# Joining the moments of two norms on GpSimd, with the square roots, reciprocals and scalings a slot or more later

## The reference

```
x  = x + layernorm(attention(layernorm(x)))        # norms 1 and 2
x  = x + layernorm(spikes(layernorm(x)))           # norms 3 and 4
_layernorm(x) = (x - mean) / sqrt(var + 1e-5)      # over the 256 features
attention: q, k, v = x @ W_qkv.T; k normalised per head (16 values);
           F_t = retention * F_(t-1) + coef * v_t k_t^T;  y_t = (W_LTM + F_t) q_t;  y @ W_o.T
spikes:    y = relu(x @ W_fc.T)^2 @ W_proj.T; five steps of a threshold neuron; spike count / 5
```

## Time and profile before

| | us |
|---|---|
| median of three runs (634.02, 634.74, 641.57) | 634.74 |
| the profiled execution's own time | 633.62 |
| its span, first to last instruction | 631.8 |
| PE busy | 497.6 (79%) |
| DVE busy | 534.2 (85%) |
| ACT busy | 328.7 (52%) |
| POOL busy | 389.0 (62%) |
| mean granted TensorE clock | 0.886 |

### The profile page before, as it was taken

The page is one execution under the profiler, slowest core; times in us unless marked ns, Lnnn a source line. Parts: engine busy times, 40 slices in busy tenths (PEclk is TensorE's granted clock), DMA queues, the critical chain, the costliest instruction groups (busy, mean ns, idle before and its releaser), DMA issues.

```text
span 631.8 us, 7778 instructions
## 1 busy us (share of the span) xinstructions
PE 497.6 (79%) x2264; PEld 325.4 (52%) x2272; DVE 534.2 (85%) x933; ACT 328.7 (52%) x641; POOL 389.0 (62%) x186
## 2 busy tenths in 40 slices
PE   3585548359996999699969997899879996896891
PEld 1341225136673667365736575566646664484670
DVE  4799999997999999999999998999999999712001
ACT  4532113245647754675466636654666455636634
POOL 0048975785567766877687756875787677710201
PEclk9877667659997999899989989799979997978896
DMA  7475566456644774466556653577347844200000
GB/s 238 112 210 144 162 154 186 131 143 160 182 133 116 188 209 137 133 167 200 149 149 152 176 170 107 147 182 206 100 117 202 215 101 133 67 1 0 33 1 33
DMA packets 54730, 87.63 MB, mean 139 GB/s; under 512 B 5409, under 2 KB 19361, under 8 KB 54689
## 3 DMA queue, kind: packets, MB, share of 16 engines
q1 hardware_dynamic: 54112, 87.12, 49.9%
q10 hardware_dynamic: 576, 0.03, 0.1%
HBM read 78.74 MB, written 8.39 MB: 138 GB/s over the span
## 4 chain that ended last, share of the span: by engine, by line
PE 51%; issue 16%; DVE 15%; ACT 10%; POOL 6%; DMA 1%; POOLq 0%; ACTq 0%; DVEq 0%
PE p_c L346 13%; PE p_c L371 12%; DVE state L732 9%; PE p_a L281 6%; PE p_y L324 5%; PE p_c L337 4%; POOL prod L873 3%; ACT sign L547 3%; PE p_c L354 2%; PE p_a L301 2%; POOL x1t L889 2%; DVE p_u L722 2%; PE p_y L319 2%; ACT oo L468 1%; PE p_c L363 1%
## 5 line engine op out<-in xcount | busy, mean ns | idle before, releaser
L873 POOL TENSOR_TENSOR prod<-state,qf 128x1024 f32<-128x1024 f32 x128 | 303.1, 2373 | 140.4 <-DVE state L732 121.9
L732 DVE TENSOR_TENSOR_SCAN state<-ret,p_u 128x512 f32<-128x512 f32 x256 | 309.2, 1209 | 0.0
L722 DVE TENSOR_TENSOR p_u<-vrep,p_k 128x512 f32<-128x512 f32 x256 | 171.5, 676 | 2.5 <-ACT p_k L479 2.5
L346 PE MATMUL p_c<-wproj_sb,ht 128*128 128x256 f32 x512 | 116.1, 382 | 1.3 <-ACT ht L537 1.3
L346 PEld LDWEIGHTS p_c<-wproj_sb,ht 128*128 128x128 f32 x512 | 95.7, 190 | 24.3 <-issue 9.2
L371 PE MATMUL p_c<-x1t,wfc_s 128*128 128x512 f32 x384 | 98.9, 410 | 9.1 <-POOL x1t L889 8.0
L281 PE MATMUL p_a<-xt,wqkv_s 128*128 128x512 f32 x276 | 82.7, 438 | 10.6 <-POOL xt L889 3.0
L371 PEld LDWEIGHTS p_c<-x1t,wfc_s 128*128 128x128 f32 x384 | 73.9, 196 | 31.3 <-POOL x1t L889 12.3
L324 PE MATMUL p_y<-prod,summer 128*32 128x512 f32 x512 | 76.8, 675 | 10.4 <-POOL prod L873 10.4
L281 PEld LDWEIGHTS p_a<-xt,wqkv_s 128*128 128x128 f32 x276 | 53.3, 203 | 45.7 <-issue 16.9
L535 ACT ACTIVATE hr<-p_c 128x512 f32<-128x512 f32 x64 | 38.2, 597 | 34.6 <-PE p_c L371 32.6
(11 more groups left out here) (107 smaller groups left out, 505.2 us busy)
## 6 DMA issues: line engine op xcount, KB each, us to landing
vrep<-v_rows SPq DMA_DIRECT2D x256, 256.0 KB, 3.6
xa<-in_x SPq DMA_DIRECT2D x8, 512.0 KB, 5.3
v_rows<-vf SPq DMA_DIRECT2D x16, 256.0 KB, 2.3
x<-in_x SPq DMA_DIRECT2D x8, 512.0 KB, 4.5
out<-x SPq DMA_DIRECT2D x8, 512.0 KB, 3.3
ht<-in_w_fc SPq DMA_DIRECT2D x1, 1024.0 KB, 7.6
wproj_sb<-in_w_proj SPq DMA_DIRECT2D x1, 1024.0 KB, 10.1
state<-in_w_qkv SPq DMA_DIRECT2D x1, 512.0 KB, 5.8
```

The lines of the kernel that those rows point to most:

```text
L346: last = pe.matmul(p_c[(u + 1) % 2][:, 0:D], ht[:, f, tokens(u)], wproj_sb[:, f, :], start=(f == 0), stop=(f == FT - 1))
L722: v.tensor_tensor(p_u[n % NU][:, :], vrep[:, n % NV, :], p_k[:, :], ALU.mult).then_inc(S["hebb_done"], 1)
L732: v.tensor_tensor_scan(state[:, s % NS, i, :], ret[:, r:r + 1].broadcast_to([P, L]), p_u[n % NU][:, :], 0.0, ALU.mult, ALU.add).then_inc(S ...
L873: p.tensor_tensor(prod[:, s % NZ, :, :], state[:, s % NS, :, :], qf[:, s // HS, :].unsqueeze(1).broadcast_to([P, 2, L]), ALU.mult).then_in ...
```

## The change

For norms 1 and 4 VectorE only takes BN_STATS. GpSimd then joins the halves over all four tiles at once, in new tiles `squares`, `spread` and `twice_mean`: the squares of both halves are added, and 64 times the squared difference of the two means is added to them. This is 256 times the variance, so that ScalarE's square root takes `scale=1/256`. These are five GpSimd instructions of 128x4 values for norm 1 and six for norm 4 (which also keeps the sum of the means); three of them wait for the one before on the semaphore `pool_step`. The spike norm's offsets become two GpSimd instructions, the second of which waits in the same way. Norms 2 and 3 stay as they are.

Moved in the lists, besides:

- GpSimd: `moments_of(1, b)` in slot 1 and `moments_of(4, b2)` in slot 11, ahead of that slot's `read`; `spike_offsets` in slot 13 ahead of the read; `add_feed_forward` from slot 13 to slot 15.
- ScalarE: `deviation(1)` from slot 0 to slot 2, ahead of `copy_y`; `norm1` from 2 to 3; `deviation(4)` from 11 to 12, now behind `hidden(b1, 1)` and `hidden(b1, 2)`; `norm4` from 12 to 14.
- VectorE: `scales(1)` from slot 2 to 3. `scales(4)` stays in slot 12.

```diff
             def deviation(n, b):
                 act.wait_ge(S[f"n{n}_var"], at(b + 1))
-                eps = eps_sb[:, 1:2] if n == 4 else eps_sb[:, 0:1]
-                nc.scalar.activation(dev[n - 1][:, :], moments[n - 1][:, :, 1], ACT.Sqrt, bias=eps).then_inc(S[f"n{n}_dev"], 1)
+                if n in (1, 4):
+                    eps = eps_sb[:, 1:2] if n == 4 else eps_sb[:, 0:1]
+                    nc.scalar.activation(dev[n - 1][:, :], squares[n][:, :], ACT.Sqrt, bias=eps, scale=1.0 / D).then_inc(
+                        S[f"n{n}_dev"], 1)
...
             def norm4(b):
-                act.wait_ge(S["n4_step"], at(2 * (b + 1)))
+                act.wait_ge(S["n4_offset"], at(b + 1))
...
+                        if after: deviation(1, b)
                         if before: copy_y(b1, 1)
                         if now: key_deviation(g, 1)
-                        if after: norm1(b)
...
                     if s == 11:
                         if now: copy_y(g, 0)
-                        if two_before: deviation(4, b2)
                         if after: square_k(b, 0)
                         if before:
                             hidden(b1, 1)
                             hidden(b1, 2)
                     if s == 12:
+                        if two_before: deviation(4, b2)
                         if after: key_deviation(b, 0)
-                        if two_before: norm4(b2)
...
+                    if s == 14 and two_before: norm4(b2)
                     if before and s == 15: hidden(b1, 5)
...
-                    if after and s == 2: scales(1, b)
+                    if after and s == 3: scales(1, b)
...
-                    if two_before and s == 12:
-                        scales(4, b2)
-                        spike_offsets(b2)
+                    if two_before and s == 12: scales(4, b2)
...
+            def moments_of(n, b):
+                pool.wait_ge(S[f"n{n}_stats"], at(b + 1))
+                pool.wait_ge(S[f"n{n}_dev"], at(b))
+                means = [stats[n - 1][:, :, i] for i in (1, 4)]
+                sums = [stats[n - 1][:, :, i] for i in (2, 5)]
+                if n == 4:
+                    p.tensor_tensor(twice_mean[:, :], means[0], means[1], ALU.add)
+                p.tensor_tensor(squares[n][:, :], sums[0], sums[1], ALU.add)
+                step(p.tensor_tensor(spread[n][:, :], means[0], means[1], ALU.subtract))
+                step(p.tensor_tensor(spread[n][:, :], spread[n][:, :], eight[:, :], ALU.mult))
+                step(p.tensor_tensor(spread[n][:, :], spread[n][:, :], spread[n][:, :], ALU.mult))
+                p.tensor_tensor(squares[n][:, :], squares[n][:, :], spread[n][:, :], ALU.add).then_inc(S[f"n{n}_var"], 1)
+            def spike_offsets(b):
+                pool.wait_ge(S["n4_step"], at(b + 1))
+                pool.wait_ge(S["n4_done"], at(TILES * b))
+                step(p.tensor_tensor(twice_mean[:, :], twice_mean[:, :], minus_half[:, :], ALU.mult))
+                p.tensor_tensor(nmr[:, :], twice_mean[:, :], rdev[3][:, :], ALU.mult).then_inc(S["n4_offset"], 1)
+            pool.wait_ge(S["halves_set"], 1)
+            moments_of(1, 0)
...
+                    if after and s == 1: moments_of(1, b)
+                    if two_before and s == 11: moments_of(4, b2)
+                    if two_before and s == 13: spike_offsets(b2)
                     if s > 0 and now: read(g, s - 1)
...
-                    if two_before and s == 13: add_feed_forward(b2)
+                    if two_before and s == 15: add_feed_forward(b2)
```

More of the change, by code:

```diff
@@ L113, in build @@
         nmr = sb("nmr", [P, TILES])
+        squares = {n: sb(f"squares{n}", [P, TILES]) for n in (1, 4)}
+        spread = {n: sb(f"spread{n}", [P, TILES]) for n in (1, 4)}
+        twice_mean = sb("twice_mean", [P, TILES])
+        eight = sb("eight", [P, TILES])
+        minus_half = sb("minus_half", [P, TILES])
         xa = sb("xa", [P, TILES, D])
@@ L596, in iteration @@
                         if now and before: copy_key(g, 0)
-                        if after: deviation(1, b)
                         if now: copy_v(g, 1)
@@ L612, in iteration @@
                         if now: copy_q(g, 1)
+                        if after: norm1(b)
                     if s == 4:
@@ L692, in scales @@
                 v.reciprocal(rdev[n - 1][:, :], dev[n - 1][:, :]).then_inc(S[f"n{n}_step"], 1)
-            def spike_offsets(b):
-                dve.wait_ge(S["n4_step"], at(2 * b + 1))
-                for u in range(TILES):
-                    last = v.tensor_scalar(nmr[:, u:u + 1], moments[3][:, u, 0:1], rdev[3][:, u:u + 1], -1.0, ALU.mult,
-                                           ALU.mult)
-                last.then_inc(S["n4_step"], 1)
             def mean_out():
@@ L846, in iteration @@
                         scan(g, s, 0)
-                    if after and s == 2: scales(1, b)
+                    if after and s == 3: scales(1, b)
                     if now and s == 4: key_reciprocal(g, 1)
-                    if before and s == 4: statistics(2, b1, oo, "o_done", 2 * (b1 + 1))
+                    if before and s == 4:
+                        statistics(2, b1, oo, "o_done", 2 * (b1 + 1))
+                        moments_of(2, b1)
                     if before and s == 5: scales(2, b1)
                     if now and s == 6: norm_k(g, 1)
-                    if before and s == 7: statistics(3, b1, x1[b1 % 2], "x1_done", b1 + 1)
+                    if before and s == 7:
+                        statistics(3, b1, x1[b1 % 2], "x1_done", b1 + 1)
+                        moments_of(3, b1)
                     if two_before and s == 10: statistics(4, b2, spk, "spk_done", 2 * (b2 + 1))
-                    if two_before and s == 12:
-                        scales(4, b2)
-                        spike_offsets(b2)
+                    if two_before and s == 12: scales(4, b2)
                     if g == 0 and s == 13: mean_out()
```

17 lines of the change are left out of this document (14 added, 3 removed).

## The result

The changed kernel takes 650.55 us, the median of four executions (649.27 to 655.79), against 638.07 for four of the kernel before on the same chip (634.02 to 641.57): a ratio of 1.0213 with a 95% interval of 1.0113 to 1.0313. It is slower, and whether by more than 2% the interval leaves open. The forecast was 646.0 us, +12.2 on the profiled execution before; the medians differ by 12.5. The two profiled executions, 633.62 and 651.8 us, differ by 18.2, and the 6 us above the forecast need an explanation of their own.

What follows compares the result with a forecast made beforehand. The prediction took TensorE and ScalarE, not busiest VectorE, to bound steady iterations (65.27 us). Terms -0.8 + 6.8 + 5.0 + 0.6 + 0.6 = +12.2 us on 633.62 gave 646 us, range 641 to 652 for 8 in 10.

Steps and rivals of the forecast that it cites:

- The root's place and VectorE's wait: Slot 12: norm 4's root, now behind two hidden tiles, leaves VectorE's reciprocal idle some 2.8 us, its next product 2.2 late.
- Who waits: Steady passages: GpSimd's reads and residual delay sums, making key_variance 1.7 us late each; four passages, +6.8 us.
- Neither of the two moves alone would cost much here, both do: Steady iterations: late root or later residual alone costs little, since without VectorE's delay GpSimd ties with sums at 228.2.
- Iteration 7 and the drain: Last recurrence iteration, where VectorE is the chain: the late root delays the last sums and everything after, +5.0 us.
- Start and end: First norm 1 and last norm 4: GpSimd's small dependent instructions lie on the chain, +0.6 us at each.
- The two joinings: Iterations 0 and 1, where VectorE is the chain: two joinings of norm 1 saved, -0.8 us.
- the first and fourth terms of the forecast: -0.8 us for joinings saved in iterations 0 and 1; +0.6 us for GpSimd's small instructions at the start.
- (a): TensorE's clock falls more often, 1.7 us each: 647.7 with one more, 653 with four; two or more, chance 0.15.
- (b): GpSimd's small instructions are dear, 0.5 us each or a slow first one: 650 to 652 us; chance 0.10.
- (c): Slack ahead of sums takes up the delay, only small terms stay: 634 us, no change; chance 0.11.
- (d): VectorE is the true bound, so 1.4 us comes off each of six iterations: about 626 us; chance 0.04.
- (e): The change doesn't do what it says, the joining could stay on VectorE; no size or chance given.

Runs made afterwards that it cites:

- e6: Kernel before without joining the moments of norms 1 and 4 (that computation left out): 635.55 us, ratio 0.9999.
- e1: Changed kernel with norm 4's square root back in ScalarE's slot 11, ahead of the key's copy: 640.18 us, ratio 1.0051.
- e2: Changed kernel with norm 4's reciprocal in VectorE's slot 13 and the offsets in GpSimd's slot 14, root still late: 643.00 us, ratio 1.0103.
- e4: Kernel before with only GpSimd's feed-forward residual addition moved from slot 13 to 15: 640.05 us, ratio 1.0045.
- e3: Kernel before with only norm 4's square root moved from ScalarE's slot 11 to 12: 654.90 us, ratio 1.0282.
- e8: Kernel before with norm 4's root late and norm 1's root, reciprocal and scaling placed as in the change: 651.36 us, ratio 1.0246.
- e9: Kernel before with norm 4's root late, norm 1's steps placed as in the change, and the residual addition in slot 15: 661.92 us, ratio 1.0415.
- e7: Changed kernel, reciprocal and offsets a slot later, residual behind state 15's read, first norm 1 and last norm 4 joined on VectorE: 636.83 us, ratio 0.9998.
- e10: Changed kernel with the residual addition moved behind the read of state 15, into GpSimd's next slot 0 (last tile's stays): 644.16 us, ratio 1.0124.

## Why the prediction was right, and where it was not

**What bounds it: right.** A saving on VectorE is worth nothing in the steady iterations: e6 took 0.8 us of VectorE's work out of each and the period stayed.

**The root's place and VectorE's wait: right.** Forecast 2.8 us, measured 3.18; no wait for `kdev`, as forecast. e1 and e2 take the wait away in two ways, and the period comes back to 65.5.

**Who waits: right, and 1.7 an iteration is 1.65.** `sums` waits 1.63 (forecast 1.9) and starts 1.92 later in the iteration (forecast 1.95; TensorE itself comes 0.28 later to it), period 66.92 (forecast 67.0). The chain read 14, residual, read 15 stands in the rows without a gap.

**"Neither of the two moves alone would cost much here, both do": wrong by half.** It holds for the residual (e4, period unchanged) and not for the root. I had tested the residual without the root, and never the root without the residual. There `sums` waits 1.11 us (e3) since state 15 itself comes late, and the kernel before has in addition a place that the changed one mends, norm 1 ahead of the output copies. The wait of 1.63 is made up so: 1.10 by the root (e8), 1.28 by the residual (e9), and 0.75 less than e9, 0.53 of it because the offsets have left VectorE and 0.21 because TensorE comes later. My working had the first of these in its chain without saying so (2.8 us of waiting, the next product only 2.2 late), against its own sentence that a saving on VectorE buys little: as soon as VectorE waits there, it is worth half a microsecond.

**ScalarE's and norm 1's moves "cost nothing": borne out.** The kernels without a delay that are built from the changed one, e1, e2 and e7, have a period of 65.5 and not 65.27; e4 and e6, built from the kernel before, have 65.25 to 65.29. The 0.23 lies in TensorE's `up` products, here eighteen of the kernel before and then of the changed one:

```profile
351.84 4.38 PE L371 MATMUL p_c<-x1t,wfc_s 128*128 128x512 f32 x18
```

```profile
224.23 4.44 PE L376 MATMUL p_c<-x1t,wfc_s 128*128 128x512 f32 x18
```

So it is in all six kernels built from the changed one (4.44 to 4.45, and 2.96 to 2.97 for twelve products) against 4.37 to 4.39 and 2.91 to 2.92 in the six others. In e2 TensorE is 0.22 us behind the kernel before at the last of them (`sums` 57.89 against 57.67 us after the start of `project_out`). e8 and e9 have norm 1's moves and the short products, so it is not these moves. What makes the products longer, the new tiles, the small steps or `norm4`'s new place, no run shows.

**Iteration 7 and the drain: right, with some luck.** The last `sums` comes 16.27 us later than before, and `project_out` of iteration 6 came 11.24 later: 5.03, forecast 5.0. (The passage it stands for is the fifth, not the sixth as the prediction calls it.) But in it are two slow products (3.4 us, which I had not booked). With them TensorE is 16.26 us late at `down` (517.13 against 500.87); 1.9 are covered on the way to `up` (14.33 late at 546.10, as late as VectorE is at norm 3), and 1.5 are regained there: eighteen products `up`, 5.99 us before at a low clock, took 4.46. That these come out even is luck. The second `hidden` is then 1.57 us later than `project_out` of iteration 6 (forecast 1.5), VectorE's next product 3.27 (forecast 3.1). From VectorE's product (552.18, 14.51 late) to `sums` (16.27 late) come 1.76 more, of the 1.9 forecast.

**Start and end: mis-sized, 0.9 each in place of 0.6.** From the statistics to the reciprocal pass 3.09 us at the start and 3.19 at the end, against 2.17 and 2.18; the offsets give back 0.07 where I had put 0.2. An instruction takes 0.20 us (forecast 0.18), but one that waits for the one before starts 0.28 after it, a hop of 0.08 and not 0.04, and from VectorE's end to GpSimd's start it is 0.14 us. The 6 us for a first call, by the Trainium skill (GPSIMD Engine Reference, Instruction dispatch), did not fall on this norm: the kernel's first product started 0.14 us after its input and took 0.20 us at 8.78, and the measurement decides. Whether code was loaded in GpSimd's idle time before that, no row shows.

**The two joinings, -0.8:** not resolved. In the profile the first `project_out` is 2.4 us later than before, not earlier, and e6, which has only the gain, shows 0.0 within 1.9.

**The sum: partly luck.** The two profiled executions lie 18.1 us apart in span. At the second `project_out` the changed one is 2.8 us late (170.72 against 167.93), where the first and fourth terms of the forecast make -0.2; from there to that of iteration 6 it loses 8.45 (forecast 6.8), for it has one slow product more on this stretch; iteration 7 adds 5.0 (forecast 5.0); behind the last `sums` come 1.8 (forecast 0.6), 0.8 of them because this `sums` itself takes 1.94 in place of 1.16 us. The 3.0 at the start are not shown to be the change's: over the twelve profiled executions the second `project_out` comes anywhere from 167.93 to 173.51 us, in e6, which only takes work away, at 171.44, and the kernel before has the earliest of all.

**Rivals.** (a), more slow products, is in part what the profiled execution shows on top: three more than before (four of six against one), of which, as reckoned above, only about one is felt at the end. The window of 5 us that holds one of them (busy time of the engines, granted clock, DMA share, GB/s):

```profile
238.00:243.00 5.00, 5.00 (x17) 4.07 (x16) 5.00 (x8) 0.70 (x2) 3.93 (x2) 0.66 1.09 290
```

Against the medians (a) is not needed: 650.55 less 638.07 is 12.5, because the kernel before has its own slower executions (641.57, 641.4), and its profiled one, with a single slow product, was among its fastest. The forecast stood on that one; counted from 638.07 it would be 650.3. With an interval of 1.0113 to 1.0313, some 6 us to either side, that the medians agree with it to 0.3 us is luck too. At the start the clock played in as well. TensorE's projections of the first batch took 2.93 us where they had taken 1.65, here TensorE's row of the changed kernel and then that of the kernel before:

```profile
25.43 2.93 PE L286 MATMUL p_a<-xt,wqkv_s 128*128 128x512 f32 x6 [1.06 <-DVE wqkv_s L805]
```

```profile
24.49 1.65 PE L281 MATMUL p_a<-xt,wqkv_s 128*128 128x512 f32 x6 [1.51 <-DVE wqkv_s L800]
```

e7, which joins the first norm 1 on VectorE, has its first `project_out` at 103.31 us but its second at 168.99, 1.06 later than before. (b) falls by the rows of 0.20 us. (c) and (d) needed the root in time: e1 has it in time, and its period is that of (c), unchanged but for the 0.23 of the `up` products, without the gain of (d). (e) falls: 94 VectorE instructions are gone.

## What to carry to other kernels

Engines with fixed lists are coupled by the position of each instruction in its list, and not by its work: a reciprocal of 0.18 us in front of a recurrence costs what its input is late, and moving it one slot on (e2) took some 7 us off. When a change has several moves, work out each alone and each pair; two that tie with the same deadline do not simply add. Relieving the busiest engine pays only where that engine is late for somebody, and that place may exist only after another move has made it late.

## What was not expected of the hardware

GpSimd does a TENSOR_TENSOR of 128x4 values in 0.20 us, the first of the kernel too; a dependent chain goes at 0.28 us a step, where it waits on a semaphore of its own. Four BN_AGGR on VectorE take 0.38 us, so five such steps are three times as long in a chain.

The same product sequence is slow (5.39 against 3.70) in one to four of six iterations of otherwise alike stretches. The kernels in which `sums` waits 1 us and more have 4, 3, 2 and 4 such, the others 1, 2, 2, 1, 2, 3, 2 and 4, one execution each: more idling tends to go with more of them, but e10 has four with a wait of 0.36, so these runs do not settle what decides. In e9, where TensorE had idled 2.38 us ahead of `sums`, the granted clock was 0.66 from 235 to 240 us, in the key's projection, and 1.00 from 240 us on, in `project_out`. Two of its four slow projections have a fast `project_out` behind them, two a slow one:

```profile
235.00:240.00 5.00, 3.82 (x18) 2.23 (x11) 5.00 (x7) 1.70 (x5) 2.44 (x2) 0.66 1.04 290
240.00:245.00 5.00, 5.00 (x27) 4.42 (x27) 5.00 (x8) 1.60 (x4) 3.94 (x2) 1.00 1.10 276
```
